# A graph layer's input loaded with eight consecutive nodes per partition

## What is computed

```
h = relu(layernorm(x))                              # x: 12500 x 64
W = einsum('rb,bio->rio', comp, basis)              # 64 relations of 64 x 64
s = segment_sum(h[src] * norm, etype * N + dst)     # R*N rows
agg = relu(einsum('rni,rio->no', s, W) + bias)
y = agg + relu(h @ res_w.T + res_b)
return x + batchnorm_over_nodes(y) * gamma + beta
```

## Time and profile before

| | |
|---|---|
| time, median of 3 runs | 1975.42 us (1975.33 to 1975.82) |
| span of the profiled execution | 2559.4 us; the profile gives no other time for it |
| busy: PE, ACT, DVE, POOL | 65%, 39%, 41%, 58% |
| HBM read, written | 80.28 MB, 226.35 MB |
| DMA busy share, first 16 of 40 slices | 0.5 to 0.8, later 0.1 |
| granted TensorE clock | 0.7 to 0.9 of 2.4 GHz in most of the first 16 slices, later mostly 0.5 |

### The profile page before, as it was taken

The page is one execution under the profiler, slowest core; times in us unless marked ns, Lnnn a source line. Parts: engine busy times, 40 slices in busy tenths (PEclk is TensorE's granted clock), DMA queues, the critical chain, the costliest instruction groups (busy, mean ns, idle before and its releaser), DMA issues. The chain is left out here.

```text
span 2559.4 us, 29252 instructions
## 1 busy us (share of the span) xinstructions
PE 1675.1 (65%) x6522; PEld 817.4 (32%) x6571; DVE 1040.2 (41%) x3394; ACT 1003.6 (39%) x2898; POOL 1474.2 (58%) x1565
## 2 busy tenths in 40 slices
PE   1267677867787767466666677768778787872223
PEld 1222222323233222244444434434434343331112
DVE  0442013335233211255555535636546363632324
ACT  0255543424343332655555526526436252610001
POOL 7265535554465553366666666666666666666664
PEclk9997878878798878555555575575565757575656
DMA  7066667767687765111111111111111111111112
GB/s 141 24 244 264 263 250 275 304 234 285 254 341 300 291 230 198 45 42 40 43 40 40 43 28 41 42 27 39 40 31 39 31 40 31 35 23 41 39 41 63
DMA packets 120893, 308.66 MB, mean 121 GB/s; under 512 B 49361, under 2 KB 49644, under 8 KB 95395
## 3 DMA queue, kind: packets, MB, share of 16 engines
q1 hardware_dynamic: 56622, 233.21, 23.4%
q0 software_dynamic: 49504, 50.79, 10.6%
q10 hardware_dynamic: 14588, 22.76, 3.2%
HBM read 80.28 MB, written 226.35 MB: 120 GB/s over the span
## 5 line engine op out<-in xcount | busy, mean ns | idle before, releaser
L618 POOL DMA_INDIRECT shared<-z_table,idx_all x1019 | 967.3, 949 | 605.8 <-issue 233.6
L590 POOL DMA_INDIRECT acc<-in_x,idx_all x520 | 493.9, 950 | 448.5 <-DMA head_rows<-acc 299.7
L1238 PE MATMUL zps<-wp,res 128*128 128x512 bf16 x1915 | 503.3, 414 | 188.8 <-issue 79.9
L655 ACT ACTIVATE zst<-zps 128x512 f32<-128x512 f32 x480 | 276.9, 599 | 365.3 <-PE zps L1238 223.1
L762 ACT ACTIVATE res<-res,hw 128x64 f32<-128x64 f32 x1056 | 357.5, 426 | 104.2 <-issue 53.8
L1371 PE MATMUL mps<-wp,res 128*128 128x160 f32 (+4 forms) x528 | 271.9, 620 | 158.7 <-issue 84.4
L1238 PEld LDWEIGHTS zps<-wp,res 128*128 128x128 bf16 x1956 | 190.1, 103 | 490.6 <-issue 164.5
L1105 DVE TENSOR_SCALAR shared<-iota,rel_all,wgt_all 128x36 f32<-128x36 f32 (+9 forms) x1035 | 307.9, 326 | 62.0 <-ACT res L729 61.5
L1356 PE MATMUL zps<-shared 128*64 128x36 f32 (+9 forms) x1354 | 208.3, 317 | 146.2 <-issue 72.7
L749 ACT ACTIVATE res<-res,hm 128x64 f32<-128x64 f32 x528 | 176.0, 334 | 224.9 <-issue 132.2
L1356 PEld LDWEIGHTS zps<-shared 128*64 128x64 f32 x1354 | 143.7, 197 | 351.6 <-issue 283.3
(11 more groups left out here) (202 smaller groups left out, 1306.9 us busy)
## 6 DMA issues: line engine op xcount, KB each, us to landing
z_table<-zst SPq DMA_DIRECT2D x194, 1024.0 KB
wp<-z_table SPq DMA_DIRECT2D x1792, 0.2 KB
head_rows<-acc SPq DMA_DIRECT2D x66, 256.0 KB
res<-head_rows ACTq DMA_DIRECT2D x64, 256.0 KB
shared<-z_table,idx_all POOLq DMA_INDIRECT x1019
acc<-in_x,idx_all POOLq DMA_INDIRECT x520
wp<-z_table ACTq DMA_DIRECT2D x256, 0.2 KB
zst<-in_x ACTq DMA_DIRECT2D x12, 256.0 KB
```

The costliest lines, as they stand in the source:

```text
L590: e.indirect_dma_start(out=ring[:, b % NRING, i, :], out_offset=None, in_=x, in_offset=bass.IndirectOffsetOnAxis(ap=idx_first[:, t:t + 1] ...
L618: e.indirect_dma_start(out=ys[:, q % NY, :], out_offset=None, in_=table[:, :], in_offset=bass.IndirectOffsetOnAxis(ap=idx_all[:, col:col + ...
L655: e.activation(to, frm, ACT.Copy).then_inc(s_ez, 1)
L1238: last = e.matmul(to, lhsT=stationary(px, pw), rhs=moving(px, pw), start=(a == 0), stop=(a == 2))
```

## The change

Partition p of tile t now holds node c*1024 + 8p + j, with chunk c = t // 8 and j = t % 8: each partition reads 8 consecutive nodes, 2 KB, in one piece (13 loads for 8 loads). The last chunk has 2 nodes for each of 106 partitions, so tiles 96 and 97 both have 106 rows, where tile 96 had 128 and tile 97 84. A table store now writes 128 pieces of 8 KB that lie 128 KB apart (16 KB before), and the four stores of tiles 96 and 97 have 106 rows. The residual's moving operand is contiguous in the node of a tile. The table itself, its gathers and the output stay as they are.

```diff
+    x_group = [min(c for c in range(NLN) if (c + 1) * LNT * P > n * EPI) for n in range(NEPI)]
...
+        def rows_of(t):
+            return TAIL_ROWS if t * P >= (NEPI - 1) * EPI else P
+
+        def nodes_of(rows, n):
+            return rows[n * EPI:min((n + 1) * EPI, N), :].rearrange("(p j) f -> p (j f)", j=epi_run[n])
...
-            for c in range(NLN):
-                t0, t1 = c * LNT, min((c + 1) * LNT, NT - 1)
-                e.dma_start(xr[:, t0:t1, :], xv[:, t0:t1, :]).then_inc(s_x[c], 16)
-            e.wait_ge(s_pad, 1)
-            e.dma_start(xr[0:LAST, NT - 1, :], x[(NT - 1) * P:N, :]).then_inc(s_x[NLN - 1], 16)
+            for n in range(NEPI):
+                if n == NEPI - 1:
+                    e.wait_ge(s_pad, 1)
+                t0 = n * EPI // P
+                e.dma_start(xr[0:rows_of(t0), t0:t0 + epi_run[n], :],
+                            nodes_of(x, n).rearrange("p (j f) -> p j f", f=F)).then_inc(s_x[x_group[n]], 16)
...
-                rows = LAST if t == NT - 1 else P
-                e.dma_start(zview[t * P:t * P + rows, h * ZT * BANK:(h + 1) * ZT * BANK],
-                            zst[0:rows, n % NZS, :, :].rearrange("p k n -> p (k n)")).then_inc(s_zst[n % NZS], 16)
+                c, j = divmod(t, EPI // P)
+                e.dma_start(nodes_of(zview, c).rearrange("p (j n) -> p j n", j=epi_run[c])[:, j, h * ZT * BANK:(h + 1) * ZT * BANK],
+                            zst[0:rows_of(t), n % NZS, :, :].rearrange("p k n -> p (k n)")).then_inc(s_zst[n % NZS], 16)
...
-                e.wait_ge(s_x[c], 32 if c == NLN - 1 else 16)
+                e.wait_ge(s_x[c], 16 * x_group.count(c))
...
-                            b[h * F:(h + 1) * F, 0:epi_width[c]].rearrange("p (q i) -> p q i", i=P)[:, :, i0:i0 + nodes // run],
+                            b[h * F:(h + 1) * F, q0:q0 + nodes // 2].rearrange("p (q i) -> p q i", i=P),
                             lambda px, pw: wp[:, pw, R, :],
-                            lambda px, pw: xp[:, ch, px, 0:nodes].rearrange("p (i q a) -> p a q i", a=2, q=run // 2)[:, h])
+                            lambda px, pw: xp[:, ch, px, 0:nodes].rearrange("p (q a i) -> p a q i", a=2, i=P)[:, h])
```

More of the change, by code:

```diff
@@ L83, in rgcn_kernel @@
     NT = math.ceil(N / P)
-    LAST = N - (NT - 1) * P
     NQ = NT // 2
@@ L476, in _ @@
         def _(e):
-            xv = x[0:(NT - 1) * P, :].rearrange("(t p) f -> p t f", p=P)
-            for c in range(NLN):
-                t0, t1 = c * LNT, min((c + 1) * LNT, NT - 1)
-                e.dma_start(xr[:, t0:t1, :], xv[:, t0:t1, :]).then_inc(s_x[c], 16)
-            e.wait_ge(s_pad, 1)
-            e.dma_start(xr[0:LAST, NT - 1, :], x[(NT - 1) * P:N, :]).then_inc(s_x[NLN - 1], 16)
+            for n in range(NEPI):
[4 more added lines that the diff above has]
+                            nodes_of(x, n).rearrange("p (j f) -> p j f", f=F)).then_inc(s_x[x_group[n]], 16)
             e.wait_ge(s_pad, 2)
@@ L696, in products @@
                     t, h = STORES[n]
-                    rows = LAST if t == NT - 1 else P
+                    rows = rows_of(t)
                     if n == NZS - 1:
@@ L803, in link @@
                 e.wait_ge(s, steps[s])
-            e.memset(xr[:, NT - 1, :], 0.0).then_inc(s_pad, 1)
+            e.memset(xr[:, NT - epi_run[-1]:NT, :], 0.0).then_inc(s_pad, 1)
             e.memset(wgt_f[64:GB, 1, :], 0.0).then_inc(s_pad, 1)
@@ L1252, in residual @@
                 b = bank(("r", c))
-                run = epi_run[c]
                 for ch in range(2 * c, min(2 * c + 2, NCH)):
                     nodes = min(BANK, NT * P - ch * BANK)
-                    i0 = (ch - 2 * c) * BANK // run
+                    q0 = (ch - 2 * c) * BANK // 2
                     for h in range(2):
                         last = three_parts(
-                            b[h * F:(h + 1) * F, 0:epi_width[c]].rearrange("p (q i) -> p q i", i=P)[:, :, i0:i0 + nodes // run],
+                            b[h * F:(h + 1) * F, q0:q0 + nodes // 2].rearrange("p (q i) -> p q i", i=P),
                             lambda px, pw: wp[:, pw, R, :],
-                            lambda px, pw: xp[:, ch, px, 0:nodes].rearrange("p (i q a) -> p a q i", a=2, q=run // 2)[:, h])
+                            lambda px, pw: xp[:, ch, px, 0:nodes].rearrange("p (q a i) -> p a q i", a=2, i=P)[:, h])
                 last.then_inc(s_pz, 1)
```

## The result

The changed kernel takes 2026.65 us, the median of four runs (2025.28 to 2028.66), against 1975.62 us before (four runs, 1975.33 to 1979.99): a ratio of 1.0252, 95% interval 1.024 to 1.0264, so 51.0 us more. Its profiled execution took 2026.19 us, 1.8 us more than its span of 2024.4.

The account below looks back on a forecast made before the run. POOL's nearly unbroken gathers were taken to bound the kernel: 1975.4 + 57 (later table) - 2 (slack) - 4 (residual) = 2026 us. The range was 2006 to 2038, with slower at 0.92.

Parts of the forecast that it names:

- Where the profiled execution's 584 us lie: Profiled span 2559.4 us against timed 1975.42: almost all of POOL's waits there were said to come with profiling.
- The match of 1966 with 1975: POOL gathering at 1.249 us without pause gives 1966 us, 9 us below the timed runs; taken as support for that pace.
- Whatever makes POOL wait is paid in full: POOL gathers nearly without pause in timed runs, so any wait added to it lengthens the run in full.
- Slack of 2 us: Before the first table gather: table lands at 663 us, 2 us before POOL's head gathers end at 665.
- Four stores on two engines, the table 57 us later: Last table stores: four of 106 rows at 17.1 us each, 68 us together; table 53 to 60 us later, taken as 57.
- Load of x 0 to 3 us, taken as 0: At the start: larger x pieces could delay POOL's wait for `idx_first` by 0 to 3 us; taken as 0.
- Pitch 0: Table stores: pitch growing from 16 to 128 KB costs 0; as a rival, pieces colliding gives 2051 us, chance 0.04.
- Residual, 4 us back: PE's contiguous residual takes 15 us for 34, freeing PE some 19 us earlier; worth 0 to 9 us, taken as 4.
- The cover that I worked out: After the residual: first head product 61 us after the last table product; POOL needs PE's tile 8 55 us after its start.
- the 9 us of idle: Gap between POOL's unbroken 1966 us and the timed runs; the most that faster PE, ACT, DVE or x load gives back.
- 57 - 2 - 4 = 51: The sum: table 57 us later, less 2 us of slack, less 4 us from the residual, added to 1975.4.
- The rival with PE as the bound of the middle stage: PE, not POOL, bounds the middle stage, so the end moves by 33 us to 2008; chance 0.08.

Follow-up runs that it names:

- gathers again: Kernel before with 40 more table gathers, one after every 25th, on a 1975 us chip: 2027.02 us against 1976.23, ratio 1.0252.
- experiment 1: Changed kernel with its four 106-row stores cut into 96 and 10 rows, against before: first run 2538.87 us (ratio 0.9936), second 1976.92 us (1.0005).
- experiments 4: Kernel before with 40 more table gathers on POOL, against before: 2619.43 us (ratio 1.0236) on a 2550 us chip, 2027.02 us (1.0252) on a 1975 us chip.
- experiment 2: Kernel before with last two tiles stored as 106 + 22 and 82 + 2 rows, against before, 2550 us chips: 2591.47 us (1.0134), 2571.61 us (1.0121).

## Why the prediction was right, and where it wasn't

**Where the profiled execution's 584 us lie: wrong.** I said they come with the profiling and that a timed run has none of them. They come with the chip, or with a condition of it: on a 2550 us chip timed runs of before take 2558.2 us too, and in after and every experiment the profiled execution takes only some 1.8 us more than its span, so profiling stretches nothing. Set against "gathers again", 317 of the 584 us lie ahead of the first table gather (990.09 against 673.25) and some 262 in the table gathers; the 299.7 us in which POOL waits for stores of head rows are gone in after. What I drew from it held for the runs that count, by the pace alone: in after POOL goes from its first to its last table gather in 2001.93 - 725.30 = 1276.6 us, 1018 steps of 1.254 us, with no wait longer than the gap, and in the second run of experiment 1 in 1276.3. The match of 1966 with 1975 was evidence about the timed runs and none about profiling; I took it for both.

**Whatever makes POOL wait is paid in full: right**, by experiments 4 (50.8 us for 40 gathers) and 1 (49.4 us of span for 49.65 us of start).

**Slack of 2 us: wrong in sign.** The table was 3.6 us late before, not 2 early. POOL could have begun with the table at 668.41 + 1.25 = 669.7, 4.7 us after my 665. The table's last store is issued at 660.0 where the plan says 657, and the table lands at 673.25, 13.3 us behind that issue and not the 6.7 us of the earlier trace rows.

**Four stores on two engines, the table 57 us later: right in kind, 5 too much.** 53 pieces of 0.302 us for my 0.32 make 64 us for my 68. And in after 11 us lie ahead of and behind them, for my 0 to 6.7, while the old four took 21.5 us and not 14.6 (990.09 - 975.5). Measured it is 52.1, just under my 53 to 60.

The Trainium skill's rule (DMA: Bandwidth & Descriptors, "Why a DMA increments its semaphore by 16 and not by 1"), the largest number of engines up to 16 that divides the rows, gives two for 106. This trace agrees, with a share of 0.13 and 53 pieces in 8 us.

**Load of x 0 to 3 us, taken as 0: right** (0.1 us). **Pitch 0: right.** From 128 to 600 us "gathers again" (pitch 16 KB) and after (128 KB) both move 401 GB/s at a share of 1.01, PE at its full clock:

```profile
128.00:600.00 472.00, 436.98 (x2043) 191.38 (x2044) 203.53 (x378) 259.36 (x480) 357.12 (x378) 1.00 1.01 401
```

The Trainium skill (DMA: Bandwidth & Descriptors, "Latency and other measured facts") lists a loss at row pitches of 512 KiB and more; at 128 KB this trace has none.

**Residual, 4 us back: wrong; 0 by the traces, and less than 2 by the times of experiment 1.** The cover that I worked out is there nearly to the microsecond: the old residual takes 33.1 us (687.11 + 3.22 - 657.27) for my 34, the first head product comes 27.4 us after it for my 27.3. But that product comes 44.5 us after POOL's first table gather, and no wait of POOL for PE follows that is longer than 0.3. By my count POOL needs it 55 us after its start, so PE had 10 us to spare, and 25 us less of residual (33.1 to 8.4, where I had 34 to 15) buy nothing that the traces show. I had given it a part of the 9 us of idle because they were there, not because a row tied them to PE.

So 57 - 2 - 4 = 51 became 52 - 0 - 0 = 52, and the total hit 51.0: three terms are off by 2 to 5 us, and they cancel. The mechanism was right, the closeness of the total was luck. The rival with PE as the bound of the middle stage is out on the 1975 us chip. On the 2550 us chip part of an added wait is hidden behind PE (experiment 2, 33 us of time for 50 of wait); that this is also the rival's 33 us shows nothing, since the changed kernel was never timed there.

No kernel here beats both. On the 1975 us chip experiment 1 equals before; on the 2550 us chips the short residual without the 106-row stores gains 0.5 to 1.0%.

## What to carry to other kernels

When a layout changes how many rows the last tile has, look at that number before its bytes: 106 rows went through two engines and took 16 us for 848 KB, where 128 rows took all engines and, at 401 GB/s, 2.6 us for 1 MB; cutting the DMA into 96 + 10 rows removed the loss. Price a DMA by its pieces on its busiest engine, and ask what lies behind the last one of a batch: 192 good stores did not matter, four at the end did. Before putting a difference between a profile and the timed runs down to profiling, time the kernel again beside a profile on the same chip.

## What the runs showed of the hardware

Two kinds of chips, or conditions of them, run this kernel 28 to 30% apart. On the 2550 us chips PE's small matmuls for W come 2 to 3 us apart with no cause that the records show, while POOL gathers; the first fence is experiment 1 on such a chip, the second the same kernel on a 1975 us chip:

```profile
20.68 0.26 PE L1233 MATMUL zps<-compT,res 64*64 64x64 f32 x1 [0.65 <-issue]
22.80 0.26 PE L1233 MATMUL zps<-compT,res 64*64 64x64 f32 x1 [1.86 <-issue]
24.91 0.26 PE L1233 MATMUL zps<-compT,res 64*64 64x64 f32 x1 [1.84 <-issue]
```

```profile
19.67 4.61 PE L1233 MATMUL zps<-compT,res 64*64 64x64 f32 x60
```

Its table stage moves 265 GB/s at a share of 0.69 there, 400 at 1.00 here (128 to 600 us, same kernel). It is not the load of x in small pieces, since this kernel has large ones. Nor is it the DMA engines alone: in the trace of before, between 968 and 980 us, while POOL waits for the table, PE works without a gap at the full granted clock and the stores move 408 GB/s:

```profile
968.00:980.00 12.00, 11.95 (x56) 5.47 (x56) 3.45 (x5) 8.14 (x14) 0.00 (x0) 1.00 1.00 408
```

The residual that takes 33 us during POOL's wait and 63 us with its gathers (experiment 2) points the same way. What it is stays open.

A cut DMA isn't free for the queue that issues it. In the second run of experiment 1 the last table issues on SP take 12.18 / 6 = 2.0 us each, and the table lands 2.4 us later than in "gathers again" (675.65 to 673.25), where one issue takes 0.33. Whether that comes from the cutting or from what is queued ahead isn't shown: head stores issued behind the last table stores take up to 3.1 us each in "gathers again" too. A queue with two engines full blocks its issuer: of the 31.20 us for three stores the second and third take 14.6 and 14.5 us, and the six head stores behind them, which have nothing to do with the table, take 28.77.
